# Macaron block on one core: token groups of 2, 4 and 2 tiles, one SiLU moved ahead, and a short GpSimd power between indirect transfers

## The chip, the cores and the metric

The kernel runs on one core of one Trainium2 chip. The metric is the device time of one execution in microseconds (us), as the median of the runs; lower is better. The kernel before takes 1942.54 us (median of 3 runs, 1938.5 to 1945.58).

## The reference

The input is x of 4 x 1024 tokens with 256 channels, all in float32. Three layers follow each other, each behind a layer normalization and with a residual sum:

- `x = x + 0.5 * ffn(layernorm(x))`
- `x = x + ssm(layernorm(x))`
- `x = x + 0.5 * ffn(layernorm(x))`, with the same weights as the first

`ffn` is a mixture of experts. A router gives 16 sigmoid scores per token; the experts lie in 4 groups, of which the 2 with the highest sum of their two best scores are kept, and of their experts the 4 best. Each token is the weighted sum of 4 gated MLPs (256 to 128 to 256, SiLU), plus 2 shared experts that all tokens pass. `ssm` projects to 1024 inner channels, convolves over 4 taps, applies SiLU, a scan with a state of 64, a gate, a layer normalization and a projection back to 256.

## The kernel before

The 4096 tokens are 8 tiles of 512, each of 4 blocks of 128 tokens. Both feed-forward layers run the same code (`ffn_block`); the attention-like layer (`attn_block`) stands between them.

**Feed-forward, the data.** Tokens of several tiles form a group: `GT = (3, 3, 2)` tiles, so groups of 12, 12 and 8 blocks. When a group's scores are known, VectorE works out for each token and each of its 4 experts a row number (`rows`), such that the rows of one expert lie together. GpSimd then writes every normalized block to DRAM by those rows: four indirect transfers a block (line 362, "scatter"). SyncE loads the sorted rows back in quads (line 290), TensorE passes them through the experts, and the results go to DRAM in order (line 295). GpSimd fetches them back by the same rows, four indirect transfers a block (line 386, "gather"), and VectorE adds the four with their weights to the block (line 639, `combine`). A group has `RP = (4*blocks + 16)//4*2` routed events, so 32, 32 and 24, together 88; each takes two tiles of 128 rows.

**Feed-forward, the order.** No planner is at work: `ffn_events` writes out one list of events, and every engine walks it. `route` is the transposes (line 762) and the router's logits (line 778) of two blocks; `shared` is the two shared experts for two blocks (lines 799 and 825); `both` is the two together; `routed` is one event of a group (lines 794, 809 and 825). In each event ScalarE copies the transposed tokens of the next event out of PSUM (line 413), computes the SiLU (lines 426 and 429) and, for routed ones, copies the result out (line 436); VectorE multiplies (lines 613 and 617), copies (line 621) or adds (line 628). Engines pass work on by semaphores alone. Between the events stand the pieces of the routing (`route_piece`), the places where the counts are made (`COUNT_AT`) and where the experts' names are packed (`PACK_AT`), the normalization of further tiles, and the combines: block b of group 0 at event 13 + 8b//5 of group 1, block b of group 1 at event 4 + 8b//5 of group 2. VectorE works in order, so a combine whose block hasn't come holds up the events behind it.

**GpSimd's queue.** Its order is fixed: six small powers (line 358, the reciprocal standard deviation of a tile), scatter of group 0 with two more such powers after its blocks 1 and 2, scatter of group 1, scatter of group 2, gather of group 0, of 1, of 2. Scatter of group 2 uses the DRAM buffer of group 0, and so waits until TensorE has transposed all of group 0's rows. A gather waits until all results of its group are stored, and each of its blocks until the buffer of four blocks has one free (a combine done). Transfers inside a burst wait for nothing.

**SyncE's queue.** In the routed events it stores each result and loads a quad ahead. The first quad of a group waits until all of that group's scatters have landed. It stands between the stores of the group before: with 24 events in a group behind the store of event 16.

**Attention-like layer.** Tiles run in a loop, 4 chunks each. At the last chunk (q = 3) ScalarE does: a copy of the convolution's next input (lines 1296 and 1298), the normalization of y (line 1317), the last SiLU of the next tile (line 1303), the SiLU of z (line 1322), and the rounding of X (line 1313).

Of the kernel before, what the change touches and what calls it, by code (L numbers as in the profile page):

```python
# [17 lines left out]
NB = TOK // P  # L18
GT = (3, 3, 2)
NG = len(GT)  # L20
# [8 lines left out]
YO = 4  # L29
GBUF = 4  # L30
PIECES_W = [(0, SH), (SH, SH + 6), (SH + 6, SH + 11), (SH + 11, NU)]
NORMALIZE_AT = {("route", 1): 2, ("route", 3): 3, ("both", 6): 4, ("both", 8): 5, ("shared", 0): 6, ("shared", 1): 7}
LATE = (10, 11)
PER = 6
# [42 lines left out]
def combine_at(g, b):  # L77

    return (13 if g == 0 else 4) + 8 * b // 5

def ffn_events():

    for r in range(0, 6):
        yield "route", r
    for r in range(6, 10):
        yield "both", r
    for r in range(10, 12):
        yield "route", r
    for r in range(0, 4):  # L90
        yield "shared", r
    for r in range(12, 16):
        yield "route", r
    for r in (4, 5):
        yield "shared", r
    for g in range(NG):
        for i in range(RP[g]):
            yield "routed", (g, i)
    for r in (12, 13, 14, 15) + LATE:
        yield "shared", r  # L100
# [7 lines left out]
def ffn_block(nc, ctx, whole, consts, label, src, dst, scratch, w, shared_sems, nth):  # L108
# [37 lines left out]
    later = sb("later", [P, GROUPS])  # L146
    half_neg = sb("half_neg", [P, SUB])
    bn = sb("bn", [P, SUB, 6])
    mv = sb("mv", [P, NT, SUB, 2])
# [34 lines left out]
    w_in = sems("w_in", len(PIECES_W))  # L184
    init_done = sem("init_done")
    filled = sems("filled", 2)
    x_in = sems("x_in", NT)
# [39 lines left out]
    at_event = {e: k for k, e in enumerate(EVENTS)}  # L227
    FINAL = [("shared", 14), ("shared", 15)] + [("shared", r) for r in LATE]
    ROUTES = [(k, n) for k, (kind, n) in enumerate(EVENTS) if kind in ("route", "both")]
    COUNT_AT = [("both", 6), ("shared", 2), ("routed", (0, 5))]  # L230
    PACK_AT = [("both", 8), ("shared", 4), ("routed", (0, 9))]
    fresh = nth == 0
# [39 lines left out]
    def _(sp):  # L272
# [45 lines left out]
        for g in range(2):  # L318
            for i in range(RP[g]):
                store_y(g, i)  # L320
                if i % 2 == 0:
                    if XQ + i // 2 < RP[g] // 2:
                        load_quad(g, XQ + i // 2)
                    else:
                        load_quad(g + 1, XQ + i // 2 - RP[g] // 2)
                if g == 1:
                    for t in range(TILE0[1]):
                        if i == min(combine_at(0, SUB * t + SUB - 1) + 3, RP[1] - 1):
                            store_tile(t)
        for i in range(RP[2]):  # L330
            store_y(2, i)
            if i % 2 == 0 and XQ + i // 2 < RP[2] // 2:
                load_quad(2, XQ + i // 2)
            for t in range(TILE0[1], TILE0[2]):
                if i == combine_at(1, SUB * (t - TILE0[1]) + SUB - 1) + 3:
                    store_tile(t)
        for t in range(TILE0[1], NT):
            if t >= TILE0[2] or combine_at(1, SUB * (t - TILE0[1]) + SUB - 1) + 3 >= RP[2]:
                store_tile(t)
        sp.wait_ge(stored, 16 * NT)  # L340

    @block.gpsimd
    def _(pool):
# [12 lines left out]
        def rstd_of(t):  # L356
            pool.wait_ge(var_ready, t + 1)
            G.tensor_tensor(rstd[:, t], var[:, t], half_neg[:], ALU.pow).then_inc(rstd_ready, 1)

        def scatter(g, b):  # L360
# [16 lines left out]
        def gather_group(g):  # L377
# [23 lines left out]
    def _(act):  # L401
# [40 lines left out]
        for k, (kind, n) in enumerate(EVENTS):  # L442
            if (kind, n) == ("route", 5):
                squash(0)
            if k + 1 < len(EVENTS):
                take_xT(k + 1)
# [13 lines left out]
    def _(dve):  # L460
# [223 lines left out]
        for k, (kind, n) in enumerate(EVENTS):  # L684
            if (kind, n) == ("route", 5):
                for i in range(3):
                    route_piece(0, i)
# [12 lines left out]
            if (kind, n) == ("both", 6):  # L700
                route_piece(0, 5)
                route_piece(0, 6)
                statistics(6)
            if (kind, n) == ("both", 7):
                statistics(7)
                route_piece(0, 7)
            if (kind, n) == ("both", 8):
                shift_of(6)
                route_piece(0, 8)
            if (kind, n) == ("both", 9):  # L710
                shift_of(7)
                route_piece(0, 9)
            if (kind, n) == ("route", 11):
                route_piece(1, 0)
            if (kind, n) == ("shared", 0):
                route_piece(1, 1)
            if (kind, n) == ("shared", 1):
                route_piece(1, 2)
            if (kind, n) == ("shared", 2):
                route_piece(1, 5)  # L720
            if (kind, n) == ("shared", 3):
# [5 lines left out]
            if (kind, n) == ("shared", 4):  # L727
                route_piece(1, 9)
# [6 lines left out]
            if (kind, n) in FINAL:  # L735
                combine(2, FINAL.index((kind, n)))
        take_part(LATE[-1], len(OUTPUTS) - 1)
        for b in range(4, GB[2]):
            combine(2, b)

    @block.tensor
    def _(pe):
# [105 lines left out]
        for k, (kind, n) in enumerate(EVENTS):  # L848
            if (kind, n) == ("route", 5):
                router(k, n)  # L850
            if k + 1 < len(EVENTS):
                turn_x(k + 1)
            if kind in ("route", "both") and n != 5:
                router(k, n)
# [31 lines left out]
def attn_block(nc, ctx, whole, consts, label, src, dst, scratch, w, used):  # L886
# [365 lines left out]
    def _(act):  # L1252
# [108 lines left out]
        def tile(t, par):  # L1361
            nx = 1 - par
            for q in range(SUB):
# [26 lines left out]
                if q < SUB - 1:  # L1390
# [551 lines left out]
```

## Time and profile before

| | us |
|---|---|
| profiled execution, its own time | 1952.48 |
| its span, first to last instruction | 1950.8 |
| first feed-forward layer, about | 0 to 651 |
| attention-like layer, about | 651 to 1298.4 |
| second feed-forward layer, about | 1298.4 to 1950.8 |

| engine | busy us | share of the span |
|---|---|---|
| TensorE (PE) | 1479.5 | 76% |
| GpSimd (POOL) | 944.6 | 48% |
| VectorE (DVE) | 890.0 | 46% |
| ScalarE (ACT) | 708.3 | 36% |

The mean granted clock of TensorE is 0.864 of full speed. The profile gives for each instruction when it ran, and for the idle time ahead of it what ended it. "remote" and "another core or an unknown queue" stand where nothing in the profile released the engine at that moment. PE is the matmuls, PEld the weight loads beside them, SPq the transfers that SyncE issues. A line such as L362 is a line of the kernel.

### The profile page before, as it was taken

To read this page: it belongs to the slowest core of one execution; us is meant where nothing else is said; L and a number is where in the kernel's file an instruction comes from. 1 tells how busy PE (TensorE), PEld (TensorE's weight loads), DVE (VectorE), ACT (ScalarE), POOL (GpSimd) and SP (SyncE) were. 2 spreads that over 40 slices of the span, in tenths; PEclk is the share of its full clock that TensorE was granted. 3 is DMA by queue.
4 is the path that set the end of the run, shared out by engine and by line. 5 is a ranking of instruction groups with operands and counts; after the bars stand their busy time and mean duration, and the time that the engine had idled before them with its cause. 6 is when DMAs were issued, how large, how long until landed. Compare 5 with 4: busy or idle time off the path is not lost. (4 is left out here: it accounts for less than half of the span.)

```text
span 1950.8 us, 24020 instructions
## 1 busy us (share of the span) xinstructions
PE 1479.5 (76%) x7430; PEld 1243.7 (64%) x7430; DVE 890.0 (46%) x2136; ACT 708.3 (36%) x1168; POOL 944.6 (48%) x980
## 2 busy tenths in 40 slices
PE   6652796599697368999999999859372994887793
PEld 5541685478586256777777777647262883776683
DVE  6340421144253557667767765546141520243343
ACT  4220342244241244555554555423120441333230
POOL 2737105433635457767767766323645016254525
PEclk9876897799799668999998998977685996899897
DMA  9722344356552400100000000033322453465533
GB/s 380 288 89 103 106 161 164 131 194 212 163 181 84 170 7 1 33 12 30 26 13 30 25 1 23 23 150 131 114 76 78 158 178 127 146 212 203 177 122 100
DMA packets 90245, 225.46 MB, mean 116 GB/s; under 512 B 16640, under 2 KB 28928, under 8 KB 89216
## 3 DMA queue, kind: packets, MB, share of 16 engines
q1 hardware_dynamic: 65536, 156.64, 22.4%
q0 software_dynamic: 24576, 67.14, 10.5%
q8 instruction: 72, 1.18, 0.2%
q14 instruction: 61, 0.50, 0.1%
HBM read 114.67 MB, written 109.05 MB: 115 GB/s over the span
## 5 line engine op out<-in xcount | busy, mean ns | idle before, releaser
L362 POOL DMA_INDIRECT xg<-f_xn,f_rows x256 | 251.0, 980 | 383.3 <-PE f_xT_ps L762 208.7
L794 PE MATMUL f_gu_ps<-f_wgu,f_xT 128*128 x1408 | 362.7, 404 | 95.7 <-issue 94.4
L386 POOL DMA_INDIRECT f_gbuf<-yg,f_rows x256 | 262.4, 1025 | 333.3 <-DVE f_xin L639 137.4
L794 PEld LDWEIGHTS f_gu_ps<-f_wgu,f_xT 128*128 128x128 f32 x1408 | 273.5, 205 | 133.9 <-issue 99.6
L825 PE MATMUL f_y_ps<-f_wd,f_hT 128*128 (+1 forms) x960 | 260.9, 402 | 121.0 <-DVE f_hT L621 67.8
L825 PEld LDWEIGHTS f_y_ps<-f_wd,f_hT 128*128 128x128 f32 x960 | 190.3, 201 | 158.2 <-issue 131.2
L613 DVE TENSOR_TENSOR f_h<-f_gu_ps,f_sg 128x256 f32<-128x256 f32 x176 | 74.7, 424 | 427.7 <-ACT f_sg L426 347.8
L413 ACT COPY f_xT<-f_xT_ps 128x512 f32<-128x512 f32 x232 | 136.2, 587 | 295.3 <-remote 148.7
L799 PE MATMUL f_gu_ps<-f_xT,f_wgu 128*128 128x256 f32 x512 | 142.2, 438 | 74.3 <-DVE f_hT L617 61.1
L426 ACT ACTIVATE f_sg<-f_gu_ps 128x256 f32<-128x256 f32 x176 | 67.9, 386 | 302.2 <-PE f_gu_ps L794 181.0
L799 PEld LDWEIGHTS f_gu_ps<-f_xT,f_wgu 128*128 128x128 f32 x512 | 111.0, 224 | 97.8 <-issue 80.1
L436 ACT COPY f_yo<-f_y_ps 128x512 f32<-128x512 f32 x176 | 103.2, 586 | 119.6 <-PE f_y_ps L825 74.8
L639 DVE SCALAR_TENSOR_TENSOR f_xin<-f_gbuf,f_w,f_xin 128x256 f32<-128x256 f32 x256 | 123.4, 483 | 11.8 <-DMA f_gbuf<-yg,f_rows 4.9
L1476 DVE SCALAR_TENSOR_TENSOR at_xs<-at_raw,at_taps,at_xs 128x512 f32<-128x512 f32 x132 | 118.7, 901 | 13.0 <-POOL at_xs L1195 9.4
L762 PE MATMUL f_xT_ps<-ident,f_xq 128*128 128x128 f32 x704 | 114.8, 289 | 3.9 <-issue 1.6
L621 DVE COPY f_hT<-f_hT_ps 128x256 f32<-128x256 f32 x176 | 74.6, 424 | 94.2 <-remote 49.4
L1702 PE MATMUL at_xu_ps<-at_wout,at_ynT_hi 128*128 128x256 f32 x512 | 104.8, 305 | 2.4 <-DVE at_ynT_lo L1485 2.4
L1194 POOL TENSOR_SCALAR at_tap<-at_raw,at_taps 128x512 f32<-128x512 f32 x60 | 98.1, 1635 | 6.0
L1232 POOL TENSOR_TENSOR at_S_split<-at_S,at_S_split 64x1024 fp32r<-64x1024 f32 x32 | 76.4, 2389 | 40.2 <-ACT at_S_split L1374 40.2
L762 PEld LDWEIGHTS f_xT_ps<-ident,f_xq 128*128 128x128 f32 x704 | 90.3, 151 | 5.2 <-issue 4.8
L617 DVE TENSOR_TENSOR f_hT<-f_gu_ps,f_sg 128x256 f32<-128x256 f32 x64 | 26.3, 423 | 145.5 <-ACT f_sg L429 91.8
L1702 PEld LDWEIGHTS at_xu_ps<-at_wout,at_ynT_hi 128*128 128x128 f32 x512 | 87.2, 208 | 6.3 <-issue 2.9
(233 smaller groups left out, 2738.0 us busy)
## 6 DMA issues: line engine op xcount, KB each, us to landing
f_xq<-xg SPq DMA_DIRECT2D x88, 512.0 KB
yg<-f_yo SPq DMA_DIRECT2D x176, 256.0 KB
xg<-f_gbuf SPq DMA_DIRECT2D x32, 512.0 KB, 15.0
f_wgu<-in_gate_up SPq DMA_DIRECT2D x4, 1280.0 KB, 19.8
f_xin<-in_x SPq DMA_DIRECT2D x8, 512.0 KB, 6.9
xg<-f_xn,f_rows POOLq DMA_INDIRECT x256
f_gbuf<-yg,f_rows POOLq DMA_INDIRECT x256
x<-f_xin SPq DMA_DIRECT2D x8, 512.0 KB
```

The costliest lines, as they stand in the source:

```text
L362: G.indirect_dma_start(xg[g], bass.IndirectOffsetOnAxis(ap=rows[g][:, b, k:k + 1], axis=0), xn[:, SUB * TILE0[g] + b, :], None, bounds_che ...
L386: G.indirect_dma_start(gbuf[:, n % GBUF, k, :], None, yg[g], bass.IndirectOffsetOnAxis(ap=rows[g][:, b, k:k + 1], axis=0), bounds_check=2 ...
L413: A.copy(xT[:, k % 2], xT_ps[:, k % 2]).then_inc(xT_ready, 1)
L436: A.copy(yo[:, n % YO, :], y_ps[:, yy % 2]).then_inc(y_out, 1)
L639: ins = V.scalar_tensor_tensor(out=xin[:, n // SUB, n % SUB, :], in0=gbuf[:, n % GBUF, k, :], scalar=w4[g][:, b, k:k + 1], in1=xin[:, n // ...
L762: last = T.transpose(xT_ps[:, k % 2, c:c + P], of[s][:, d * P:(d + 1) * P], ident[:])
L794: last = T.matmul(gu_ps[:, j % 2, s * 2 * P:(s + 1) * 2 * P], x_of(k, s, d), weight(wgu[:, :, d, :], experts[s]), start=(d == 0), stop=(d ...
L799: last = T.matmul(gu_ps[:, j % 2, half * 2 * P:(half + 1) * 2 * P], wgu[:, experts[0], d, half * P:(half + 1) * P], xT[:, k % 2, 2 * d * P ...
L825: last = T.matmul(y_ps[:, yy % 2, s * D:(s + 1) * D], hT[:, i % 4, s * P:(s + 1) * P], weight(wd, experts[i][s]), start=(i == units[0]), s ...
L1194: link(G.tensor_scalar(tap0[:], raw[:, j % 2, 0:TILE], taps[:, j, 0:1], None, ALU.mult))
L1476: ins = V.scalar_tensor_tensor(out=acc, in0=raw[:, j % 2, k:k + TILE], scalar=taps[:, j, k:k + 1], in1=acc, op0=ALU.mult, op1=ALU.add)
L1702: nc.tensor.matmul(xu_ps[:, 0, 0:D], ynT_hi[:, j, :], wout[:, j, i, :], start=(j == 0 and i == 0), stop=False)
```

## The change

- The groups have 2, 4 and 2 tiles, that is 8, 16 and 8 blocks, with 24, 40 and 24 routed events; together 88 as before.
- The list of events, and what stands between the events, is laid out anew for these groups. Eight shared events now stand at the end instead of six, and the combines of the last blocks of group 1 stand there too.
- GpSimd gets `rest()`: a power over 128 x 4 elements and a wait for its own completion. It stands ahead of the first and the third transfer of each block, in all scatters and gathers, but for the very first transfer of a group.
- In the attention-like layer, the last SiLU of the next tile moves up at q = 3, ahead of the copy and of the normalization of y.

```
-GT = (3, 3, 2)
+GT = (2, 4, 2)
+REST_SCATTER = (0, 1, 2)
+REST_GATHER = (0, 1, 2)
+REST_EVERY = 2
-NORMALIZE_AT = {("route", 1): 2, ("route", 3): 3, ("both", 6): 4, ("both", 8): 5, ("shared", 0): 6, ("shared", 1): 7}
-LATE = (10, 11)
+NORMALIZE_AT = {("both", 4): 3, ("both", 6): 4, ("both", 7): 5, ("shared", 8): 6, ("shared", 9): 7}
+LATE = (2, 3, 10, 11)
 def combine_at(g, b):
-    return (13 if g == 0 else 4) + 8 * b // 5
+    return (12 if g == 0 else 4) + 8 * b // 5
 def ffn_events():
     # before: route 0-5, both 6-9, route 10-11, shared 0-3, route 12-15, shared 4-5,
     #         routed, shared 12 13 14 15 10 11
     # after:  route 0-3, both 4-7, route 8-11, shared 8 9 0 1, route 12-15,
     #         routed, shared 2 3 12 13 14 15 10 11
...
+    LAST = [(1, 13), (1, 14), (1, 15)] + [(2, b) for b in range(GB[2])]
...
+        def rest():
+            rests[0] += 1
+            G.tensor_tensor(idle[:], ones_m[:, 0:SUB], half_neg[:], ALU.pow).then_inc(rested, 1)
+            pool.wait_ge(rested, rests[0])
...
         def scatter(g, b):
             for k in range(4):
+                if g in REST_SCATTER and k % REST_EVERY == 0 and b + k:
+                    rest()
                 G.indirect_dma_start(xg[g], ...).then_inc(scattered[g], 16)
...
                 for k in range(4):
+                    if g in REST_GATHER and k % REST_EVERY == 0 and b + k:
+                        rest()
                     G.indirect_dma_start(gbuf[:, n % GBUF, k, :], None, yg[g], ...)
...
             if (kind, n) in FINAL:
-                combine(2, FINAL.index((kind, n)))
+                combine(*LAST[FINAL.index((kind, n))])
...
                 else:
+                    if more(t, 1):
+                        silu_x(t + 1, nx, 2 * q + 1)
                     if more(t, 2):
                         copy_xp(t + 2, par, 0)
                     normalize_y(c)
                     if more(t, 1):
-                        silu_x(t + 1, nx, 2 * q + 1)
                         silu_z(c + 1)
                         round_X(c + 1)
```

## Rows read from the trace of the kernel before

**Rows 1.** Stretches: start:end, length, busy us of engines (instructions), PE clock, DMA, GB/s.
```profile
0.00:651.00 651.00, 454.74 (x2226) 390.05 (x2226) 235.71 (x757) 190.09 (x367) 270.38 (x295) 0.85 0.49 173
...
1298.40:1950.80 652.40, 458.05 (x2226) 392.90 (x2226) 234.98 (x752) 187.43 (x365) 265.32 (x267) 0.82 0.42 147
```

**Rows 2.** Stretches of line 362 alone, the scatters: POOL busy (transfers), PE clock, DMA.
```profile
50.10:113.70 63.60, 47.23 (x48) 0.78 0.62 239
1344.50:1408.20 63.70, 47.34 (x48) 0.75 0.27 97
1435.50:1497.00 61.50, 47.05 (x48) 0.67 0.28 100
1601.00:1641.90 40.90, 31.22 (x32) 0.71 0.42 151
```

**Rows 3.** The same of line 386, the gathers.
```profile
593.40:641.90 48.50, 32.73 (x32) 0.89 0.34 106
1649.90:1757.30 107.40, 49.19 (x48) 0.89 0.56 183
1780.30:1864.20 83.90, 49.17 (x48) 0.86 0.54 178
1891.30:1943.60 52.30, 33.06 (x32) 0.79 0.32 98
```

**Rows 4.** Timeline, scatter of group 1: start, length, engine, instruction, [idle before <-releaser].
```profile
1453.53 0.95 PE L762 MATMUL f_xT_ps<-ident,f_xq 128*128 128x128 f32 x4
...
1488.38 0.59 ACT L413 COPY f_xT<-f_xT_ps 128x512 f32<-128x512 f32 x1 [29.01 <-remote]
1503.09 0.38 ACT L426 ACTIVATE f_sg<-f_gu_ps 128x256 f32<-128x256 f32 x1 [14.12 <-remote]
```

**Rows 5.** Timeline of POOL, a small power between the transfers of scatter 0.
```profile
1353.79 0.97 POOL L362 DMA_INDIRECT xg<-f_xn,f_rows  x1 [0.30 <-issue]
1354.76 1.08 POOL L358 TENSOR_TENSOR f_rstd<-f_var,f_half_neg 128x4 f32<-128x4 f32 x1
1356.03 1.05 POOL L362 DMA_INDIRECT xg<-f_xn,f_rows  x1 [0.19 <-issue]
```

**Rows 6.** Timeline of PE and ACT behind those powers: transposes, and the copy that waits for them.
```profile
1354.86 0.73 PE L762 MATMUL f_xT_ps<-ident,f_xn 128*128 128x128 f32 x4 [2.36 <-DVE f_words L589]
1356.75 0.59 ACT L413 COPY f_xT<-f_xT_ps 128x512 f32<-128x512 f32 x1 [5.68 <-PE f_xT_ps L762]
1365.99 0.63 PE L762 MATMUL f_xT_ps<-ident,f_xn 128*128 128x128 f32 x4
1366.66 0.59 ACT L413 COPY f_xT<-f_xT_ps 128x512 f32<-128x512 f32 x1 [0.70 <-PE f_xT_ps L762]
```

**Rows 7.** Timeline of DVE and POOL: transfers behind a wait, and beside combines.
```profile
1927.02 2.04 DVE L639 SCALAR_TENSOR_TENSOR f_xin<-f_gbuf,f_w,f_xin 128x256 f32<-128x256 f32 x4
1929.82 1.00 POOL L386 DMA_INDIRECT f_gbuf<-yg,f_rows  x1 [6.98 <-DVE f_xin L639]
...
1939.44 1.26 POOL L386 DMA_INDIRECT f_gbuf<-yg,f_rows  x1 [0.30 <-issue]
```

**Rows 8.** Timeline: two routed events in steady state, and the gather behind that group.
```profile
1767.16 1.89 PE L794 MATMUL f_gu_ps<-f_wgu,f_xT 128*128 x8
1770.41 0.81 PE L794 MATMUL f_gu_ps<-f_wgu,f_xT 128*128 x3
...
1780.40 1.00 POOL L386 DMA_INDIRECT f_gbuf<-yg,f_rows  x1 [23.17 <-DMA yg<-f_yo]
```

**Rows 9.** Timeline of DVE and ACT at q = 3 of a tile.
```profile
795.87 1.53 DVE L1476 SCALAR_TENSOR_TENSOR at_xs<-at_raw,at_taps,at_xs 128x512 f32<-128x512 f32 x2
797.15 0.59 ACT L1296 COPY at_raw<-at_mm_ps 128x512 f32<-128x512 f32 x1 [3.13 <-PE at_mm_ps L1640]
799.43 0.62 ACT L1303 ACTIVATE at_xs<-at_xs 128x512 f32<-128x512 f32 x1
802.29 1.22 DVE L1538 TENSOR_TENSOR at_X_lo<-at_xu_ps,at_X_hi 128x1024 fp32r<-128x1024 f32 x1 [4.89 <-ACT at_X_hi L1313]
```

More of the change, by code:

```diff
@@ L77, in combine_at @@
 def combine_at(g, b):
-    return (13 if g == 0 else 4) + 8 * b // 5
+    return (12 if g == 0 else 4) + 8 * b // 5
 def ffn_events():
-    for r in range(0, 6):
+    for r in range(0, 4):
         yield "route", r
-    for r in range(6, 10):
+    for r in range(4, 8):
         yield "both", r
-    for r in range(10, 12):
+    for r in range(8, 12):
         yield "route", r
-    for r in range(0, 4):
+    for r in (8, 9, 0, 1):
         yield "shared", r
@@ L93, in ffn_events @@
         yield "route", r
-    for r in (4, 5):
-        yield "shared", r
     for g in range(NG):
@@ L98, in ffn_events @@
             yield "routed", (g, i)
-    for r in (12, 13, 14, 15) + LATE:
+    for r in (2, 3, 12, 13, 14, 15, 10, 11):
         yield "shared", r
@@ L147, in ffn_block @@
     half_neg = sb("half_neg", [P, SUB])
+    idle = sb("idle", [P, SUB])
     bn = sb("bn", [P, SUB, 6])
@@ L185, in ffn_block @@
     init_done = sem("init_done")
+    rested = sem("rested")
     filled = sems("filled", 2)
@@ L227, in ffn_block @@
     at_event = {e: k for k, e in enumerate(EVENTS)}
-    FINAL = [("shared", 14), ("shared", 15)] + [("shared", r) for r in LATE]
+    FINAL = [("shared", r) for r in (2, 3, 12, 13, 14, 15, 10, 11)]
+    LAST = [(1, 13), (1, 14), (1, 15)] + [(2, b) for b in range(GB[2])]
+    EARLY = [(g, combine_at(g, SUB * (t - TILE0[g]) + SUB - 1) + 3, t) for g in range(2)
+             for t in range(TILE0[g], TILE0[g + 1]) if 2 * t + 1 not in LATE]
+    EARLY = {(g + 1, i): t for g, i, t in EARLY if i < RP[g + 1]}
+    AT_END = [t for t in (4, 1, 6, 5, 7) if t not in EARLY.values()]
     ROUTES = [(k, n) for k, (kind, n) in enumerate(EVENTS) if kind in ("route", "both")]
-    COUNT_AT = [("both", 6), ("shared", 2), ("routed", (0, 5))]
-    PACK_AT = [("both", 8), ("shared", 4), ("routed", (0, 9))]
+    COUNT_AT = [("both", 4), ("shared", 0), ("routed", (0, 5))]
+    PACK_AT = [("both", 6), ("routed", (0, 1)), ("routed", (0, 9))]
     fresh = nth == 0
@@ L325, in _ @@
                         load_quad(g + 1, XQ + i // 2 - RP[g] // 2)
[L326 to L329, printed above, removed]
+                if (g, i) in EARLY:
+                    store_tile(EARLY[g, i])
         for i in range(RP[2]):
@@ L333, in _ @@
                 load_quad(2, XQ + i // 2)
[L334 to L339, printed above, removed]
+            if (2, i) in EARLY:
+                store_tile(EARLY[2, i])
+        for t in AT_END:
+            store_tile(t)
         sp.wait_ge(stored, 16 * NT)
@@ L358, in rstd_of @@
             G.tensor_tensor(rstd[:, t], var[:, t], half_neg[:], ALU.pow).then_inc(rstd_ready, 1)
+        rests = [0]
+        def rest():
+            rests[0] += 1
+            G.tensor_tensor(idle[:], ones_m[:, 0:SUB], half_neg[:], ALU.pow).then_inc(rested, 1)
+            pool.wait_ge(rested, rests[0])
         def scatter(g, b):
             for k in range(4):
+                if g in REST_SCATTER and k % REST_EVERY == 0 and b + k:
+                    rest()
                 G.indirect_dma_start(xg[g], bass.IndirectOffsetOnAxis(ap=rows[g][:, b, k:k + 1], axis=0),
@@ L442, in _ @@
         for k, (kind, n) in enumerate(EVENTS):
-            if (kind, n) == ("route", 5):
+            if (kind, n) == ("route", 3):
                 squash(0)
+                normalize(2)
             if k + 1 < len(EVENTS):
@@ L684, in _ @@
         for k, (kind, n) in enumerate(EVENTS):
-            if (kind, n) == ("route", 5):
+            if (kind, n) == ("route", 3):
                 for i in range(3):
@@ L699, in _ @@
                     copy_words(g, k)
-            if (kind, n) == ("both", 6):
+            if (kind, n) == ("both", 4):
                 route_piece(0, 5)
@@ L703, in _ @@
                 statistics(6)
-            if (kind, n) == ("both", 7):
+            if (kind, n) == ("both", 5):
                 statistics(7)
                 route_piece(0, 7)
-            if (kind, n) == ("both", 8):
+            if (kind, n) == ("both", 6):
                 shift_of(6)
                 route_piece(0, 8)
-            if (kind, n) == ("both", 9):
+            if (kind, n) == ("both", 7):
                 shift_of(7)
@@ L714, in _ @@
                 route_piece(1, 0)
+            if (kind, n) == ("shared", 8):
+                route_piece(1, 1)
+            if (kind, n) == ("shared", 9):
+                route_piece(1, 2)
             if (kind, n) == ("shared", 0):
-                route_piece(1, 1)
+                route_piece(1, 5)
             if (kind, n) == ("shared", 1):
[L718 to L721, printed above, removed]
                 route_piece(1, 6)
@@ L726, in _ @@
                 route_piece(1, 8)
-            if (kind, n) == ("shared", 4):
+            if (kind, n) == ("routed", (0, 0)):
                 route_piece(1, 9)
@@ L735, in _ @@
             if (kind, n) in FINAL:
-                combine(2, FINAL.index((kind, n)))
-        take_part(LATE[-1], len(OUTPUTS) - 1)
-        for b in range(4, GB[2]):
-            combine(2, b)
+                combine(*LAST[FINAL.index((kind, n))])
+        take_part(FINAL[-1][1], len(OUTPUTS) - 1)
+        for g, b in LAST[len(FINAL):]:
+            combine(g, b)
     @block.tensor
@@ L848, in _ @@
         for k, (kind, n) in enumerate(EVENTS):
-            if (kind, n) == ("route", 5):
+            if (kind, n) == ("route", 3):
                 router(k, n)
@@ L852, in _ @@
                 turn_x(k + 1)
-            if kind in ("route", "both") and n != 5:
+            if kind in ("route", "both") and n != 3:
                 router(k, n)
```

## The prediction

> **What bounds the kernel now.** I read the stretches first. Each feed-forward layer takes about 651 us, and the PE is busy for 455 to 458 of it at a granted clock of 0.82 to 0.85 [rows 1]. So some 195 us of each layer are idle on the PE, and the low clock adds more. The bursts of GpSimd's indirect transfers show where: in the scatters of the second layer the clock is 0.67 to 0.75, so the PE hardly works there, though the transfers keep the DMA engines only 27 to 42% busy [rows 2].
>
> The timeline of one such burst shows the reason. The PE ends its transposes at 1453.53 + 0.95 = 1454.48. ScalarE, which only has to copy them, starts at 1488.38 and was idle for 29.01 us, "remote" [rows 4]. What the transposes signal arrives 34 us late. The burst ends at 1497.0 [rows 2], and the next SiLU, whose matmuls were over by 1454, starts at 1503.09 [rows 4]: six us after the last transfer everything held up is let go. In the quiet stretches the same hop takes hundredths of a us: transposes end at 1366.62, the copy starts at 1366.66 [rows 6]. So while transfers follow each other with no pause, what the PE signals gets through late, and the longer the burst the later.
>
> Two places in the trace have a pause. After eight transfers stands a small power of 1.08 us [rows 5]; the transposes that end beside it, at 1355.59, are answered at 1356.75, 1.16 us late; further on, behind the second power, those that end at 1366.62 are answered after 0.04 us [rows 6]. A power between transfers does clear the way. That is what `rest()` repeats.
>
> The Trainium skill has a rule that speaks against this cause: "SBUF — State Buffer", in "SBUF: two separate sides", says that it is GpSimd's making of descriptors that starves while VectorE holds the shared port, so harm runs from VectorE to the transfers. By that rule a rest would help nobody, and the time would be that of rival 3. The trace agrees with it only in small: a transfer beside a combine takes 1.26 us instead of 1.00 [rows 7]; the 34 us run the other way.
>
> **What a rest costs.** Transfers of a scatter start every 0.98 + 0.30 = 1.28 us (61.5 us for 48 [rows 2]); those of a gather every 1.00 + 0.30 = 1.30 [rows 7]. The power takes 1.08 and starts where the transfer ends; with no wait behind it the next transfer starts 0.19 later [rows 5], so a power alone costs 1.08 + 0.19 - 0.30 = 0.97. But `rest()` waits for the power. So a rest costs 1.06 + 0.76 - 0.30 = 1.52; bounds 0.97 (as if nothing were lost by the wait) and about 1.75 (each of the two transfers behind it 0.08 longer, as the one at 1356.03 is [rows 5], and the power stretched a little by VectorE). I take 1.52, since the wait is of the very kind that rows 7 show. There are two a block but none at a group's first transfer: 2*32 - 3 = 61 in the scatters, 61 in the gathers, so 122 a layer and 185 us of GpSimd's time.
>
> **The layer after, by GpSimd's chain** (second layer, us from 1298.4). With signals prompt, the PE needs 3.25 us a routed event (1770.41 - 1767.16 [rows 8]), 88 of them 286 us, and it is GpSimd that is late:
>
> - Scatter 0 starts at 46.1 now. Routing needs 8 blocks instead of 12, two route events fewer lie ahead of it, but tile 2 is now normalized behind the scores: 43.5.
> - Scatter 0: 63.7 [rows 2] - 16*1.28 + 15*1.52 = 66.0, to 109.5. Rows of group 1 are ready by about then, as the events ahead of them are the same in number.
> - Scatter 1: 61.5 + 16*1.28 + 31*1.52 = 129.1, with 0.5 of wait to 239. Group 0's 24 events (78 us) are done beside it, by 200.
> - The PE then waits for group 1's rows. SyncE stands at the first quad of group 1, behind the store of event 16; the stores behind it hold only buffers that nobody needs yet. For the last landings, the quad's load and event (0,23) I allow the 10 us that a store and its landing take from event (2,0) to the gather [rows 8], an estimate: event (1,0) is at about 249, and the PE was idle for some 50 us.
> - Scatter 2: 40.9 + 15*1.52 = 63.7, to 303. What it waits for, the transposes of group 0, is long done.
> - Gather 0: 32*1.30 + 15*1.52 = 64.5, to 368.6. A block takes 8.2 us, and combines stand every 1.6 events (5.2 us), so from event (1,12), at 292 without a wait, VectorE follows the gather: block 7 is there at 371, event (1,23). The PE is two events ahead and has 14 left to (2,0): 374 + 14*3.25 = 420.
> - Gather 1 starts 10.0 us after (2,0) (1780.40 - 1770.41 [rows 8]): 430. It takes 64*1.30 + 31*1.52 = 130.5, to 561.
> - Gather 2: 64.5, to 626; transfers beside combines are up to 0.26 longer [rows 7], 3 us in all by estimate: 629. The eight shared events at the end run beside the last 80 us of the gathers, hidden: they need less, as the six of now fit beside a gather 2 of 52 us [rows 3].
> - From the last transfer to the end 7.2 us (1950.8, the span, less 1943.6 [rows 3]): 636.
>
> That is 652.4 - 636 = 16 us less. In the first layer the scatter starts 4 us later after its beginning (50.1 against 46.1 [rows 2]), and the last gather now ends at 641.9 [rows 3]; after, 629 + 4 = 633, so 8 us less. What the PE no longer waits for comes back on GpSimd's chain: the six bursts sum to 410 us of the layer now [rows 2, 3], to 66.0 + 129.1 + 63.7 + 64.5 + 130.5 + 64.5 + 3 = 521 after; the waits between them shrink from 189 to 65.
>
> **The SiLU moved up** costs or gains nearly nothing. The convolution that it waits for ends at 795.87 + 1.53 = 797.40, and the copy ahead of which it is put started at 797.15, after 3.13 us idle [rows 9]. So the copy and the normalization of y start 0.8 us later, the SiLU's result is there 1.4 us earlier for the transposes, and rounding X stays where it is, as the SiLU of z ends ahead of it within 0.1 us of now; the subtraction at 802.29 [rows 9] follows it. 7 tiles, each between -1.1 and +0.8: I take 0, between -8 and +6.
>
> **Sum.** 1952.5 (the profiled execution) - 16 - 8 + 0 = 1928.5. That execution lies 10 us above the median of the runs (1942.5); against the median the forecast is 1918.5, and as some transfers behind a power are longer [rows 5] I say 1920.
>
> **Rivals.**
> 1. *A rest is cheap* (0.97): the wait's 0.76 is hidden somehow. 0.55 * 122 = 67 us a layer less: about 1785. For it: rows 5. Against: the wait in rows 7, and in `rest()` nothing can be prepared behind the wait. A part of it, or more gained on the PE than I see, would lie between 1785 and 1895.
> 2. *A rest is dear, and GpSimd's chain eats the gain* (slower). All 244 rests lie on the chain; the gain of 24 us is gone at 0.10 us more per rest. At 1.72 (powers and transfers stretched by VectorE's work, the 1.05 for 0.98 of rows 5 and the 1.26 for 1.00 of rows 7) it is 0.2 * 244 = 49 us more: 1967.
> 3. *Rests don't clear the signals* (slower): the two powers in the trace stood by chance where the PE signalled little. Then the 24 events of group 0 can't run beside scatter 1 (the clock of 0.67 there shows how little runs now [rows 2]), they come behind it, and scatter 2 waits for them: 24*3.25 = 78 us a layer, 1920 + 156 = 2076. Against it: rows 6.
>
> **How the numbers follow.** A difference of 0.3% (6 us) is what a measurement of this kernel can tell from none: 1937 to 1948. Chances: forecast 0.57 (1895 to 1950; 0.46 of it faster, 0.09 the same, 0.02 slower), rival 1 and its parts 0.16, rival 2 0.20 (0.02 of it the same), rival 3 0.07. Faster 0.62, same 0.11, slower 0.27. The range leaves out rival 3 and the whole of rival 1: 1845 to 1972; the forecast's own is 1895 to 1950.
>
> **What would show it.** In the profile after: copies of line 413 start within 1.2 us of the PE's transposes in all bursts (step 1); transfer, transfer, power, with 0.76 us from the power's end to the next transfer (step 2); GpSimd busy without a stop from about 1342 to 1667 and from 1728 to the end, with one idle stretch of some 60 us ahead of gather 1; the PE idle for about 50 us ahead of event (1,0). I am wrong if GpSimd idles for long in more places, if a rest costs below 1.4 or above 1.65, or if "remote" waits of over 5 us are left in the bursts.

## The result, and the profile after

The changed kernel takes 1957.01 us (median of 4 runs, 1955.15 to 1958.9), the kernel before in the same comparison 1940.52 (1935.15 to 1945.58): a ratio of 1.0079, 95% interval 1.0041 to 1.0117. It is slower, by 0.8%, where 1920 and thus a faster kernel was forecast. The profiled execution took 1958.9, its span is 1957.2.

The three layers of the changed kernel, by stretches (columns as in [rows 1]):

```profile
0.00:655.30 655.30, 447.75 (x2226) 386.87 (x2226) 232.93 (x757) 191.60 (x367) 406.06 (x411) 0.85 0.49 172
655.30:1307.90 652.60, 570.72 (x2978) 463.90 (x2978) 423.09 (x622) 331.27 (x437) 410.84 (x422) 0.91 0.08 26
1307.90:1957.20 649.30, 439.62 (x2226) 380.59 (x2226) 233.07 (x757) 190.09 (x365) 402.13 (x393) 0.84 0.43 147
```

The second feed-forward layer is 3.1 us shorter than in [rows 1], not 16; the first is 4.3 us longer by these stretches. Their borders are not quite the same in the two traces. Between the same instructions (the first of the attention-like layer, at 649.05 before and 655.26 after, and the first statistics of the layer behind it, at 1302.52 and 1312.81) the first layer is 6.2 us longer, the attention-like one 4.1 longer and the second 3.9 shorter. GpSimd (the fifth busy figure) went from 265 to 402 us in the second.

The scatters and then the gathers of the second layer, the transfers alone (they answer to [rows 2, 3]):

```profile
1350.70:1418.80 68.10, 33.09 (x32) 0.88 0.17 61
1419.10:1550.70 131.60, 64.26 (x64) 0.81 0.41 146
1551.00:1615.90 64.90, 32.09 (x32) 0.92 0.65 223
...
1616.20:1683.50 67.30, 33.60 (x32) 0.78 0.46 145
1746.60:1881.10 134.50, 66.98 (x64) 0.91 0.47 155
1881.50:1949.90 68.40, 34.07 (x32) 0.77 0.25 77
```

The waits that the trace marks "remote" add up to 496 us before and to 5.5 after. The granted clock in the three scatters rose from 0.75, 0.67 and 0.71 to 0.88, 0.81 and 0.92: the PE works beside them. The timeline of the long scatter says why (PE and ACT, then the end of group 0; it answers to [rows 4, 6]):

```profile
1467.63 0.60 PE L779 MATMUL f_xT_ps<-ident,f_xq 128*128 128x128 f32 x4
1468.07 1.89 PE L811 MATMUL f_gu_ps<-f_wgu,f_xT 128*128 x8
1468.27 0.59 ACT L429 COPY f_xT<-f_xT_ps 128x512 f32<-128x512 f32 x1
...
1556.54 1.11 PE L779 MATMUL f_xT_ps<-ident,f_xq 128*128 128x128 f32 x4 [49.77 <-DMA f_xq<-xg]
```

The copy starts 0.04 us after the transposes end, 49 us into a burst of 132. Then the PE waits 49.77 us for the first rows of group 1. Both were forecast. What wasn't is the price of a rest, on the timeline of GpSimd (it answers to [rows 5, 7]):

```profile
1555.15 1.04 POOL L376 DMA_INDIRECT xg<-f_xn,f_rows  x1 [0.79 <-POOL f_idle L369]
1556.50 0.97 POOL L376 DMA_INDIRECT xg<-f_xn,f_rows  x1 [0.30 <-issue]
1557.48 1.05 POOL L369 TENSOR_TENSOR f_idle<-ones,f_half_neg 128x4 f32<-128x4 f32 x1
1559.32 1.04 POOL L376 DMA_INDIRECT xg<-f_xn,f_rows  x1 [0.79 <-POOL f_idle L369]
```

From transfer to transfer over a rest it is 1559.32 - 1555.15 = 4.17 us for two transfers, against 2 x 1.28 = 2.56 without: a rest is 1.61, made of 1.05 for the power, 0.79 behind it less the usual 0.30, and 0.07 because the transfer behind a power takes 1.04 instead of 0.97.

### The profile page after: what moved, and what is told of

Same layout as the page of the kernel before. It is cut to its first block and busy times, and to the rows that moved or that the text cites. A ratio compares the mean times of both kernels' runs of the same rounds, so it can differ in the third digit from the quotient of the medians.

```text
span 1957.2 us, 24263 instructions
## 1 busy us (share of the span) xinstructions
PE 1458.1 (75%) x7430; PEld 1231.4 (63%) x7430; DVE 889.1 (45%) x2136; ACT 713.0 (36%) x1168; POOL 1219.0 (62%) x1224
## 5 line engine op out<-in xcount | busy, mean ns | idle before, releaser
L402 POOL DMA_INDIRECT f_gbuf<-yg,f_rows x256 | 270.3, 1056 | 269.4 <-issue 111.3
L376 POOL DMA_INDIRECT xg<-f_xn,f_rows x256 | 258.5, 1010 | 172.0 <-POOL f_idle L369 96.0
L811 PE MATMUL f_gu_ps<-f_wgu,f_xT 128*128 x1408 | 346.2, 390 | 0.0
L811 PEld LDWEIGHTS f_gu_ps<-f_wgu,f_xT 128*128 128x128 f32 x1408 | 264.7, 198 | 30.7
L369 POOL TENSOR_TENSOR f_idle<-ones,f_half_neg 128x4 f32<-128x4 f32 x244 | 258.0, 1057 | 4.1
L816 PE MATMUL f_gu_ps<-f_xT,f_wgu 128*128 128x256 f32 x512 | 132.8, 417 | 23.2 <-DVE f_hT L634 22.4
L816 PEld LDWEIGHTS f_gu_ps<-f_xT,f_wgu 128*128 128x128 f32 x512 | 105.8, 213 | 41.9 <-issue 21.9
L1494 DVE SCALAR_TENSOR_TENSOR at_xs<-at_raw,at_taps,at_xs 128x512 f32<-128x512 f32 x132 | 124.9, 948 | 13.0 <-POOL at_xs L1212 9.4
```

Of the source, the lines that this page charges most:

```text
L369: G.tensor_tensor(idle[:], ones_m[:, 0:SUB], half_neg[:], ALU.pow).then_inc(rested, 1)
L402: G.indirect_dma_start(gbuf[:, n % GBUF, k, :], None, yg[g], bass.IndirectOffsetOnAxis(ap=rows[g][:, b, k:k + 1], axis=0), bounds_check=2 ...
L811: last = T.matmul(gu_ps[:, j % 2, s * 2 * P:(s + 1) * 2 * P], x_of(k, s, d), weight(wgu[:, :, d, :], experts[s]), start=(d == 0), stop=(d ...
L816: last = T.matmul(gu_ps[:, j % 2, half * 2 * P:(half + 1) * 2 * P], wgu[:, experts[0], d, half * P:(half + 1) * P], xT[:, k % 2, 2 * d * P ...
L1494: ins = V.scalar_tensor_tensor(out=acc, in0=raw[:, j % 2, k:k + TILE], scalar=taps[:, j, k:k + 1], in1=acc, op0=ALU.mult, op1=ALU.add)
```

## Experiments

Each run was timed beside the kernel before on the same chip, and the chips are of two kinds. On some the kernel before takes about 1940 (here "late chips": number 9, number 11, and the one of the result above), on others 1607 ("prompt chips": numbers 2, 5, 6). Times are medians in us; the ratio is to the kernel before as timed beside it. Below, a pause is the time from one transfer's end to the next one's start, whatever GpSimd does in it.

| run | kernel | chip | time | before | ratio, 95% |
|---|---|---|---|---|---|
| e1 | after, no rests | 6 | 1583.5 | 1607.0 | 0.9846 (0.9827 to 0.9866) |
| e2 | groups of 3, 3, 2 and old SiLU, with rests | 6 | 1928.6 | 1607.0 | 1.1997 (1.1974 to 1.2019) |
| e3 | after, SiLU back | 6 | 1951.3 | 1607.0 | 1.2141 (1.2117 to 1.2166) |
| e4, e7 | after, late wait | 6, 5 | 1806.6, 1804.9 | 1607.0, 1606.6 | 1.1227, 1.1239 |
| e12 | the same | 11 | 1805.3 | 1945.5 | 0.926 (0.9216 to 0.9305) |
| e5 | before | 5 | 1606.8 | 1606.6 | 1.0002 (0.9989 to 1.0015) |
| e6 | after | 5 | 1954.6 | 1606.6 | 1.2161 (1.2137 to 1.2186) |
| e8 | after, memset for the power | 5 | 1709.4 | 1606.6 | 1.0628 (1.0601 to 1.0655) |
| e11 | the same | 11 | 1707.9 | 1945.5 | 0.876 (0.8719 to 0.8802) |
| e9 | after, no rests, SiLU back | 9 | 1941.0 | 1940.6 | 1.0007 (0.9983 to 1.003) |
| e10 | after, memset, late wait | 9 | 1951.7 | 1940.6 | 1.0032 (0.9999 to 1.0066) |
| e13, e16 | memset every 4th, SiLU back | 2 | 1645.1, 1644.1 | 1606.6, 1606.0 | 1.0242, 1.0246 |
| e14, e17 | memset every 8th, SiLU back | 2 | 1609.1, 1608.3 | 1606.6, 1606.0 | 1.0012, 1.0008 |
| e18 | the same | 9 | 1933.3 | 1951.9 | 0.9898 (0.9856 to 0.9939) |
| e15 | before with memset rests | 2 | 1726.8 | 1606.6 | 1.0739 (1.0715 to 1.0763) |

**e1: no rests.**

```
-REST_SCATTER = (0, 1, 2)
-REST_GATHER = (0, 1, 2)
+REST_SCATTER = ()
+REST_GATHER = ()
```

> The changed kernel without any rest; groups of 2, 4 and 2 tiles and the moved SiLU stay. Theory A (the rests clear the signals, but their 244 x 1.61 to 1.7 us lie on GpSimd's chain and eat what they gain): the signals are late again in the bursts (a transpose answered after more than 20 us in the long scatter of group 1), the six bursts of a layer fall from 536 us to about 410 to 430, and the two effects cancel: 1935 to 1965, within 1% of the changed kernel. Rival B (the rests are a clear gain and the grouping is what costs): without them 1985 or more. Rival C (the grouping alone is the gain and the rests are pure cost): 1925 or less.

By its number this is rival C's, but no theory had meant a fifth less, and the reason was in its neighbour: the kernel before, 1940 in the result above, took 1607 here.

**e2: rests in the old grouping; e3: the SiLU back** behind `normalize_y(c)`, as before the change.

> The kernel before (groups of 3, 3 and 2, SiLU in its old place) with the same rests in all bursts, 244 of them. Theory A: scatter 0 takes about 63.7 - 2*1.28 + 24*1.6 = 98 us instead of 64, and with nothing to do beside it all of its rests are lost; the PE's work beside scatter 1 gains; about 1960 to 1990, slower than the changed kernel, because only the grouping with a short first group keeps the lost part small. Rival B (the grouping costs): faster than the changed kernel, 1945 or less. If the sum is right that groups don't matter: within 5 us of the changed kernel less 4 us for the SiLU.

> The changed kernel with the last SiLU of a tile back behind the normalization of y; nothing else. Theory A2 (the moved SiLU costs the 4 us by which the attention-like layer is longer, 652.6 against 648.5): 4 us faster than the changed kernel, about 1953, all of it between the two feed-forward layers. Rival (the layer is longer for another reason, such as the clock or the transfers of the first layer's last stores): within 1 us of the changed kernel.

e2 was 1928.6, 23 us below e3, which has the other grouping: with a rest's price as it is, the groups of 2, 4 and 2 tiles don't help, they cost. Theory A had it the other way round, and rival B is right for dear rests. This was on a prompt chip; on a late one e2 never ran. As the changed kernel takes the same on both kinds (e6 below), an estimate for e2 there is 1930, half a percent below the kernel before. e3 was 1951.3, 3.3 below e6 on another chip. The traces settle it better. From the attention-like layer's first instruction to the first statistics of the layer behind it, the 8 usable profiles with the SiLU moved up take 653.3 to 661.4 us, mean 657.5; the 11 with it in its old place 651.7 to 656.0, mean 654.0. The moved SiLU costs 3.5 us by these means, with a standard error of 0.9; the two ranges overlap.

**e5, e6: both kernels again, unchanged.**

> The kernel before, word for word, with a profile of its own, because its median was 1940.5 us beside the changed kernel and 1607.0 us beside the first four experiments. Theory E (whether the PE's signals are held up in bursts depends on the chip or its condition, not on the kernel): where it takes about 1607 the copies behind transposes start within a few us in all bursts and the burst of group 1's scatter has the PE working beside it; where it takes about 1940 the trace is that of the rows above. Rival F (the delay is always there, and something else, such as the granted clock in the attention-like layer, makes the 334 us): the copy beside the scatter of group 1 is again 30 us late, and the 334 us lie elsewhere.

> The changed kernel, word for word, on the same chip as the kernel before of this call. Theory E: about 1955 wherever it runs, since with rests the signals are prompt anyway and GpSimd's chain sets the time; so a ratio of about 1.22 where the kernel before takes 1607, and of 1.01 where it takes 1940. Rival F: a ratio of 1.01 everywhere.

Theory E holds. The kernel before on chip 5, by stretches (the two feed-forward layers, then the scatter of group 1) and by timeline of PE and ACT inside that scatter:

```profile
0.00:480.40 480.40, 416.74 (x2226) 367.18 (x2226) 235.99 (x757) 190.66 (x366) 269.79 (x288) 0.96 0.66 234
...
1130.00:1609.20 479.20, 421.19 (x2226) 371.45 (x2226) 235.72 (x752) 189.47 (x365) 264.96 (x268) 0.91 0.58 200
...
1240.30:1301.70 61.40, 54.13 (x281) 47.43 (x282) 29.62 (x125) 21.34 (x42) 47.03 (x48) 0.91 0.64 227
```
```profile
1256.45 0.60 PE L762 MATMUL f_xT_ps<-ident,f_xq 128*128 128x128 f32 x4
1256.65 0.38 ACT L426 ACTIVATE f_sg<-f_gu_ps 128x256 f32<-128x256 f32 x1 [1.14 <-PE f_gu_ps L794]
...
1257.08 0.59 ACT L413 COPY f_xT<-f_xT_ps 128x512 f32<-128x512 f32 x1
```

Each feed-forward layer takes 480 us instead of 651, the whole difference. The same 48 transfers take 61.4 us as in [rows 2], but the PE ran 281 instructions beside them, 92 in the burst of [rows 2], and the copy follows its transposes by 0.03 us, where it took 34 in [rows 4]. So the delay is a property of the chip (or its condition), and on a prompt chip there is nothing for a rest to clear. The changed kernel is 1955 to 1957 on either kind: 1.22 times the kernel before on the one, 1.008 on the other.

**e9: the grouping alone, on a late chip.** The edits of e1 and e3 together.

> The changed kernel without rests and with the SiLU back in its place: of the change only the groups of 2, 4 and 2 tiles are left. Where the kernel before takes about 1607 (its signals are prompt): 1579, as the rests cost 370 us (1954.6 to 1583.5) and the moved SiLU 3.3 us (1951.3 against 1954.6). Rival (the SiLU's 3.3 us are noise or hang on the rests): 1583 to 1584. Where the kernel before takes about 1940 (its signals are late in bursts): the grouping has one burst of 64 transfers, 82 us, instead of 48 and 61 us, so later signals and about 1930 to 1990; there the rests would be worth nothing or up to 40 us.

1941.0 against 1940.6. On this late chip the grouping is worth nothing by itself (to 0.3%); on prompt ones, where e1 still had the moved SiLU, 1.5%. The stretch of its scatter of group 1, and the delay inside it:

```profile
1414.20:1495.70 81.50, 21.02 (x84) 16.50 (x81) 13.91 (x46) 6.40 (x11) 62.26 (x64) 0.66 0.32 111
```
```profile
1434.22 1.99 PE L811 MATMUL f_gu_ps<-f_wgu,f_xT 128*128 x8 [1.87 <-issue]
1455.08 0.38 ACT L442 ACTIVATE f_sg<-f_gu_ps 128x256 f32<-128x256 f32 x1 [21.11 <-issue]
```

PE busy 21 of 81.5 us, a SiLU 18.9 us behind its matmuls. With the rests the same burst takes 131.6 and the PE does the group's 24 events beside it.

**e4, e7, e12: a power without the wait for its completion.** The scratch `idle` has two buffers here.

```
-            G.tensor_tensor(idle[:], ones_m[:, 0:SUB], half_neg[:], ALU.pow).then_inc(rested, 1)
-            pool.wait_ge(rested, rests[0])
+            if rests[0] > 2:
+                pool.wait_ge(rested, rests[0] - 2)
+            G.tensor_tensor(idle[:, rests[0] % 2], ones_m[:, 0:SUB], half_neg[:], ALU.pow).then_inc(rested, 1)
```

> The changed kernel with two scratch buffers for the power, and each rest waits for the rest two before it, which is long over, instead of for its own power; as many powers and waits. Theory A (a rest's price is on GpSimd's chain; of its 1.61 us some 0.6 are the sequencer that can't prepare the transfer behind the wait): a rest falls to about 1.0, pairs of transfers from 4.17 to 3.55 us, the signals stay prompt, and 122 rests a layer less 6 for the chain's idle parts give 0.6*230 = 138 us less, some of it given back where the PE becomes the bound: 1820 to 1880. Rival D (it is the pause behind the power, in which the sequencer has nothing under way, and not the power that lets the signals through): the rests are cheaper but a transpose is answered late again, over 5 us, and the time is 1900 or more.

> The kernel with the wait for the rest two before once more, for a profile in which the PE runs at its usual pace (its first profile had matmuls of 678 ns instead of 384 and 2837 us, against 1800 to 1811 in its other runs). Theory A: 1800 to 1811; a rest costs 1.0 us (two transfers and a power in 3.55 us instead of 4.17), and transposes are answered within 1.2 us. Rival D: late answers of over 5 us in the long burst.

> The power with the wait for the rest two before, once more, for a chip with late signals. Theory P (a pause in which nothing is under way is needed): GpSimd's queue always has the next work ready, so signals are late in the bursts as with the memset without its wait, and the time is 1850 to 2000. Theory Q (a power of 1.05 us between transfers is enough by itself): signals prompt and 1805 there too. Where the kernel before takes about 1607 this run repeats 1805.

1805 on all three chips, 15 below what e4 expected. GpSimd's timeline in e12:

```profile
1380.68 1.07 POOL L371 TENSOR_TENSOR f_idle<-ones,f_half_neg 128x4 f32<-128x4 f32 x1
1381.93 1.04 POOL L377 DMA_INDIRECT xg<-f_xn,f_rows  x1 [0.19 <-issue]
1383.28 1.06 POOL L377 DMA_INDIRECT xg<-f_xn,f_rows  x1 [0.30 <-issue]
1384.36 1.05 POOL L371 TENSOR_TENSOR f_idle<-ones,f_half_neg 128x4 f32<-128x4 f32 x1
```

The next transfer starts 0.19 after the power instead of 0.79. The same 244 powers stand there, each about 0.6 cheaper, and 150 us are gone (1957 to 1805): the chain of GpSimd sets the time. The signals stay prompt ("remote" waits of 5.4 us in all of e12): theory P of e12 is wrong. (The profile of e4 is left aside: that one execution took 2837 us, its matmuls 678 ns instead of 384; the other six took 1800 to 1811.)

**e8, e11: a memset for the power**, with the wait for it kept.

```
-            G.tensor_tensor(idle[:], ones_m[:, 0:SUB], half_neg[:], ALU.pow).then_inc(rested, 1)
+            G.memset(idle[:], 0.0).then_inc(rested, 1)
```

> The changed kernel with a memset over the same 128 x 4 elements in place of the power; the wait for it stays. Theory A: a rest is what the other instruction and the wait take, so it falls by the power's 1.05 less the memset's 0.1 to 0.65 us, 244 * 0.95 = 232 us off GpSimd's chain, and some of it is given back where the PE is the bound: 1720 to 1800. If the time is unchanged at about 1955, the price is not in the power. If the signals are late again (over 5 us beside the long scatter), the length of the pause matters and not that there is another instruction.

> The memset in place of the power, with the wait for it, once more, for a chip on which the PE's signals are late in bursts (the kernel before takes about 1940 there; where it takes about 1607 this run repeats 1709). Theory P (it is a pause in which GpSimd has nothing under way that lets the signals through; the wait makes one, of about 1.2 us between two transfers instead of 0.3): signals prompt in all bursts and 1709 to 1720 there too, 12% below the kernel before. Theory Q (the pause must be filled by something as long as the power, or be as long as its 2.1 us): signals late, 1900 to 1960.

1709 and 1708: on the late chip 12.4% faster than the kernel before. The stretch of the scatter of group 1 in e11, and its timeline:

```profile
1280.10:1379.90 99.80, 79.68 (x432) 70.27 (x432) 42.79 (x161) 38.07 (x71) 65.98 (x95) 0.91 0.55 191
```
```profile
1322.34 0.97 POOL L376 DMA_INDIRECT xg<-f_xn,f_rows  x1 [0.30 <-issue]
1323.30 0.13 POOL L369 MEMSET f_idle<- 128x4 f32 x1
1323.36 0.63 PE L779 MATMUL f_xT_ps<-ident,f_xq 128*128 128x128 f32 x4 [0.68 <-DVE f_words L606]
1324.02 0.59 ACT L429 COPY f_xT<-f_xT_ps 128x512 f32<-128x512 f32 x1 [1.07 <-PE f_xT_ps L779]
1324.20 1.03 POOL L376 DMA_INDIRECT xg<-f_xn,f_rows  x1 [0.78 <-POOL f_idle L369]
1325.53 0.97 POOL L376 DMA_INDIRECT xg<-f_xn,f_rows  x1 [0.30 <-issue]
```

Between transfers 1324.20 - (1322.34 + 0.97) = 0.89 us of pause instead of 0.30, once in two; two transfers and a rest in 1325.53 - 1322.34 = 3.19, so 0.6 a rest; the copy is prompt. So the power isn't needed: a pause of 0.89 us ahead of every second transfer is enough. Nor must GpSimd stand idle in it: in e12 a power fills 1.07 of the 1.25 us (1381.93 - 1380.68). What e11, e12 and the changed kernel share is more time between transfers.

**e10: both edits**, a memset and the late wait.

> The changed kernel with a memset in place of the power, and a wait for the rest two before instead of its own: as good as no pause. Where the kernel before takes about 1607: the price of a rest adds up from its parts, 1.52 us a rest in the time (371 us over 244) less 1.01 for the power (245/244) less 0.61 for the wait (150/244) is below nothing, so the two overlap; 1585 to 1610, near the kernel without rests. If it stays above 1650 there is a price in having another instruction at all. Where the kernel before takes about 1940: prompt signals (a time below 1700) would show that another instruction clears them and not a pause; late ones (above 1850), that a pause of some length is needed.

On the late chip 1951.7, no better than without rests (e9, which has the SiLU back, 1941.0). Its timeline in the long scatter:

```profile
1445.86 0.13 POOL L371 MEMSET f_idle<- 128x4 f32 x1
1446.18 0.97 POOL L377 DMA_INDIRECT xg<-f_xn,f_rows  x1 [0.19 <-issue]
1447.45 0.97 POOL L377 DMA_INDIRECT xg<-f_xn,f_rows  x1 [0.30 <-issue]
...
1489.49 0.10 POOL L371 MEMSET f_idle<- 128x4 f32 x1 [1.64 <-remote]
...
1495.07 0.59 ACT L430 COPY f_xT<-f_xT_ps 128x512 f32<-128x512 f32 x1 [16.21 <-remote]
```

The memset fits into the usual 0.30 (0.13 + 0.19), transfers still start every 1.28 (1.37 on average over this burst), and the signals are late. Another instruction alone, if it is this short, clears nothing. And not the PE's signals alone are late: the memset at 1489.49 has nothing to wait for but the signal of the memset two before it, which ended at 1481.63 + 0.13 = 1481.76, 7.7 us earlier. The prediction spoke of the PE's signals only.

**e13 to e18: rarer rests, and the old grouping.** Memset with its wait, SiLU back; `REST_EVERY = 4` in e13 and e16, and 8 in e14, e17 and e18, with this edit in the scatter and its like in the gather:

```
-                if g in REST_SCATTER and k % REST_EVERY == 0 and b + k:
+                if g in REST_SCATTER and (4 * b + k) % REST_EVERY == 0 and b + k:
```

> Groups of 2, 4 and 2, SiLU in its old place, memset with its wait ahead of every fourth transfer instead of every second: 61 rests a layer instead of 122. A memset rest costs (1709 - 1583)/244 = 0.52 us of the time. Theory R (one pause lets through all that waits, so half as many do): signals held up for at most 4 transfers, 5 us; 1704 - 122*0.52 = 1641 on any chip, plus up to 15 where signals are late. Theory S (each two transfers need their pause, what is held up piles up): 1750 or more where the kernel before takes about 1940.

> The same with a rest ahead of every eighth transfer, 29 or so a layer. Theory R: 1704 - 186*0.52 = 1607 where signals are prompt; where they are late each hop of the PE may wait for up to eight transfers, 10 us, with two or three hops in an event of 3.25 us, so the 24 events beside the scatters stretch: 1640 to 1720, no longer better than every fourth. Theory S: 1850 or more there.

> Groups of 2, 4 and 2, SiLU in its old place, memset with its wait every eighth transfer. Where the kernel before takes about 1607: 1608 to 1609, the third time. Where it takes about 1940: theory R (a pause lets through all that waits) 1640 to 1720; theory S (what is held up piles up between rare pauses) 1850 or more.

On prompt chips the sum was right to 4 us (1645, 1609), in part by luck: it counted 61 and 29 rests a layer, and the kernels have 58 and 26 (116 and 52 memsets in the traces), with which it gives 1637 and 1604. e16 and e17, the same two kernels again on the same chip, repeated the times, as was expected of them. On the late chip every eighth gives 1933, theory S. Timeline of e18:

```profile
1423.39 3.62 PE L811 MATMUL f_gu_ps<-f_wgu,f_xT 128*128 x8
1430.43 0.13 POOL L369 MEMSET f_idle<- 128x4 f32 x1
1431.34 0.97 POOL L376 DMA_INDIRECT xg<-f_xn,f_rows  x1 [0.78 <-POOL f_idle L369]
...
1439.07 0.38 ACT L442 ACTIVATE f_sg<-f_gu_ps 128x256 f32<-128x256 f32 x1 [12.16 <-remote]
```

The matmuls end at 1427.01, a full pause stands from 1430.43 to 1431.34, and the SiLU still waits until 1439.07. So here one pause doesn't let through what waits, and the time says the same of the whole. A pause ahead of every second transfer suffices, every eighth doesn't; every fourth never ran on a late chip and stays open.

e15 is the kernel before with e8's memset rests.

> The kernel before (groups of 3, 3 and 2, SiLU in its old place) with memset rests and their wait ahead of every second transfer. With pow rests the same grouping took 1928.6 against 1951.3 for groups of 2, 4 and 2 with the SiLU in its old place, 23 us less; without rests on a chip with prompt signals it is 1607 against about 1580, 27 us more. Half way between (a memset rest costs a third of a pow rest): 1695 to 1725, so no gain from either grouping (within 1% of 1704). If the grouping only pays with cheap rests: above 1730.

1726.8, 2 above the 1695 to 1725 expected and 17 above e8, which even had the moved SiLU (e8 ran on chip 5, where the kernel before takes the same 1606.6). So the grouping pays where rests are cheap (17 and the SiLU's 3.5) or absent (e1 against e5, 23 and 3.5) and costs 23 where they are dear (e3 against e2), all on prompt chips.

## Why the prediction was wrong

**Its base was right for the chip of the trace.** The late signals are real there, rests clear them, and all that was said of the order of the bursts came: the wait of 49.8 us (forecast 50), group 0 done beside scatter 1, one idle stretch of GpSimd ahead of gather 1 (63 us, forecast 61), 7.3 us of tail. Rival 3 is out. The time even lies in the wide range, 1845 to 1972; it moved the wrong way.

**The step that failed is "what a rest costs".** The term was 1.52. The bursts of the second layer measure it: 198.5 us longer than the same bursts without rests (534.8 against 42.9 + 81.5 + 40.6 in e9 and 43.2 + 85.3 + 42.8 in e1), over 122 rests, 1.63 each. The parts were in the rows before: 1.08 for the power, 0.76 and not 0.30 behind it, and 0.08 because the transfer behind a power is longer [rows 5, 7], together 1.62. I put the last part into the upper bound and left it out of the value, and the sum had 1.06 where the row has 1.08. The prediction itself said that 0.10 more a rest takes the gain. It is 0.11: 13 us a layer. The bursts sum to 534.8 where 521 was forecast. The sign of being wrong, "above 1.65", was set too wide for this: the sum was wrong before it showed.

**By layers**, between the same instructions, the first is 6.2 us longer where the sum had 8 less: 14, the same 13 and 1 of other causes. The second is 3.9 shorter where it had 16: 12, the same 13 less 1.

**"The SiLU moved up costs or gains nothing"** was wrong by 3.5 us (4.1 in these two profiles), inside its bounds. Which of its neighbours pays for it no run tells apart.

The terms add up: 1928.5 + 14 + 12 + 4 = 1958.5, and the profiled execution took 1958.9. It is rival 2's mechanism at a lower price (1.63 where it had 1.72). The prediction never priced the grouping by itself; under these rests it costs 23 us (e3 against e2, on a prompt chip), about as much as the gain that was forecast.

**From the profiled execution to the median.** A second term was mis-sized here. The forecast took 10 us off its 1928.5, because the profiled execution of the kernel before lay 10 above the median. But the 1928.5 was built from GpSimd's chain, whose length doesn't vary like that: the changed kernel's executions take 1955.15 to 1958.9, the profiled one 1.9 above the median. That is 8 of the 37 us between 1920 and 1957; the other 30, less the 1.5 that the forecast had added to 1918.5, are the terms above. Two slips in the sum weigh less and go the other way: gather 0 ends at 367.3 by its own terms, not 368.6, and the first layer's gain is 8.9, not 8, so it should have forecast 3 to 4 us less.

**Where the expected gain went.** On the late chip the PE no longer loses time to late signals, but GpSimd's bursts grew from about 410 to 535 us a layer, and they are the chain that ends last. That this chain sets the time is shown by e12 and e11: rests cheaper by 0.6 and by 1.0 us took off 152 and 249 us, about 244 times as much. Rival 1 had it so: at 0.97 a rest it gave 1785, and e12, where a rest costs 1.0, took 1805.

**What no view of one trace could show** is that the ground of the argument holds on some chips alone. On prompt ones the six bursts without a pause don't hold the PE, and 244 rests cost (1954.6 - 1583.5)/244 = 1.52 us each of the time. That this is the 1.52 of the forecast is chance: it is a rest's share of the time there, not its length.

## What to carry to other kernels

When a fix adds a fixed cost to the engine that will then be the bound, multiply what is doubtful in its price by its count before trusting the sign: here 0.1 us x 244 was all of the gain. Ask what part of the fix does the work: longer pauses did, not the power, and a memset with its wait turned 1.008 into 0.876 on a late chip. And time such a fix on more than one chip: e11 is the best version where signals are late, but on prompt chips it is 6% slower than before, and there leaving out the rests altogether (0.985) is best. Of what ran, nothing is best on both; a rest every eighth transfer was nowhere slower by more than 0.1% (1.001 on chip 2, 0.990 on chip 9). The 0.990 is in part a drift: beside e18 the kernel before took 1951.9, beside e9 on the same chip 1940.6, by which e18 would be 0.996.

## What the runs showed of the hardware

- Two kinds of chip: 1607 and about 1940 for one and the same kernel, as signals are prompt or late in a burst of GpSimd's transfers. Chips 2 and 9, each timed at two times, stayed of their kind. "Remote" waits add up to 455 to 499 us in the four late traces (before, e9, e10, e18) and to 5.4 to 6.4 in after, e11, e12 and e5. The traces differ elsewhere too, on the page's list of DMA issues. Kernel before on the late chip and then on chip 5:

```profile
f_wgu<-in_gate_up SPq DMA_DIRECT2D x4, 1280.0 KB, 19.8
```
```profile
f_wgu<-in_gate_up SPq DMA_DIRECT2D x4, 1280.0 KB, 21.5
```

  All 7 profiles of late chips have 19.2 to 19.8 us to landing there, the 13 of prompt ones 21.0 to 21.5. Why, and what makes a chip late, no run shows.
- On late chips, signals were late where the transfers of group 1's scatter started every 1.28 to 1.37 us on average (e9, e18, e10) and prompt at 1.56 and more (e11, e12, after). Whether it is the mean pace or the density of pauses isn't told apart.
- A rest of 0.6 us (e11) clears the signals as one of 1.6 (after) does. The Trainium skill says of a finished instruction ("GPSIMD Engine Reference", "2.1 Instruction dispatch") that its completion holds up only what waits on its semaphore, not the next GpSimd instruction. The traces agree: 0.19 us from a power to the next transfer with nothing to wait for (e12), 0.79 behind the wait.
- The transfers' own pace tells nothing of a delay: the scatter of 48 takes 61.5 us on the late chip and 61.4 on the prompt one. The Trainium skill says why the record may not show one, in "Perfetto Trace Analysis", "DMA Instruction — SWDGE (GPSIMD)": the recorded end of such a transfer is when its descriptors are written, not when the data has moved. No row here shows what happens behind that point.
